# A four-layer graph network on one core: where the exponential stands in ScalarE's order of the attention pass

## The reference

```python
def _top_p_attention(X, W1, W2, W3):
    q = X @ W1.T @ W2.T
    k = X @ W3.T
    probs = softmax(q @ k.T, axis=-1)                  # 5000 x 5000
    # keep the largest probabilities of each row until their sum reaches 0.9
    ...
    return A / A.sum(-1, keepdims=True)

R = S + eye(N);  R = R / R.sum(-1)                     # S is the adjacency
for n in range(2):
    A  = _top_p_attention(Xa, W1, W2, W3)
    Xf = R @ Xf                                        # "diffusion"
    Xa = A @ Xa                                        # "attention"
    Z  = Z + Xf @ U1[n].T + Xa @ U2[n].T
h = X + Z                                              # then layer norm, gain and bias
```

## Time and profile before

| what | value |
|---|---|
| device time, median of 3 runs | 7562.4 us |
| device time, lowest and highest | 7555.11 and 7564.21 us |
| device time of the profiled execution | 7571.29 us |
| its span, first to last instruction | 7569.5 us |
| granted PE clock, mean over the span | 0.830 |
| first attention pass, about | 747 to 1984 us |
| second attention pass, about | 2153 to 5397 us |

### The profile page before, as it was taken

One profiled execution on the slowest core, in us unless ns is written; L12 is line 12 of the kernel. 1 busy time (PEld: TensorE's weight loads), 2 busy tenths in 40 slices (PEclk: granted clock), 3 DMA queues, 4 the chain that ended last, 5 costly groups with the idle time before them and its releaser, 6 DMA issues. The chain is left out here.

```text
span 7569.5 us, 83686 instructions
## 1 busy us (share of the span) xinstructions
PE 4816.2 (64%) x27812; PEld 3349.8 (44%) x27812; DVE 5526.4 (73%) x13021; ACT 2216.4 (29%) x2953; POOL 297.3 (4%) x170
## 2 busy tenths in 40 slices
PE   5994888888674365524375477753316888853981
PEld 2442566666554354413264466643312222212981
DVE  4883677777348888887877778778445999974864
ACT  2332555555310011101032233321204222212541
POOL 0000000000110000000000000000000210220000
PEclk9996788888888697867687788877658999986995
DMA  5550000000032121201111111110011333312850
GB/s 173 200 201 19 1 2 1 2 1 1 26 121 88 54 90 72 80 28 42 53 69 45 39 69 70 69 52 31 21 36 65 109 103 114 109 57 75 301 186 27
DMA packets 192724, 549.73 MB, mean 73 GB/s; under 512 B 20026, under 2 KB 77125, under 8 KB 192125
## 3 DMA queue, kind: packets, MB, share of 16 engines
q1 hardware_dynamic: 187069, 539.58, 20.0%
q0 software_dynamic: 5120, 3.97, 0.2%
HBM read 526.73 MB, written 16.68 MB: 72 GB/s over the span
## 5 line engine op out<-in xcount | busy, mean ns | idle before, releaser
L647 PE MATMUL ps<-ident,arena 125*125 125x125 f32 x3200 | 544.1, 304 | 1223.4 <-DVEq L1098 1223.4
L655 PE MATMUL ps<-arena,turned 125*125 125x129 f32 x6400 | 951.0, 299 | 196.8 <-ACT turned L750 196.8
L679 PE MATMUL ps<-arena 125*125 125x129 f32 x6400 | 833.3, 290 | 318.7 <-DMA arena<-in_adj_tiles 311.6
L647 PEld LDWEIGHTS ps<-ident,arena 125*125 125x125 f32 x3200 | 475.6, 217 | 1262.5 <-DVEq L1098 1236.6
L750 ACT ACTIVATE turned<-ps 125x500 f32<-125x500 f32 x800 | 463.5, 585 | 1876.0 <-PE ps L647 1875.2
L1382 DVE SCALAR_TENSOR_TENSOR arena<-arena,pair 125x1000 f32<-125x1000 f32 x800 | 939.3, 1250 | 71.0 <-ACT arena L1345 71.0
L655 PEld LDWEIGHTS ps<-arena,turned 125*125 125x125 f32 x6400 | 876.8, 210 | 209.8 <-ACT turned L750 205.4
L679 PEld LDWEIGHTS ps<-arena 125*125 125x125 f32 x6400 | 781.3, 199 | 391.0 <-DMA arena<-in_adj_tiles 307.4
L1400 PE MATMUL ps<-arena 125*64 125x500 f32 x3200 | 763.8, 601 | 193.9 <-DVE arena L1382 193.9
L640 PE MATMUL ps<-arena,wt 64*125 64x500 f32 x1600 | 724.9, 608 | 11.0 <-ACT wt L728 9.5
L1064 DVE SCALAR_TENSOR_TENSOR arena<-arena,wt 125x5000 f32<-125x5000 f32 x80 | 434.1, 5427 | 311.6 <-issue 311.6
(11 more groups left out here) (343 smaller groups left out, 5904.3 us busy)
## 6 DMA issues: line engine op xcount, KB each, us to landing
arena<-in_adj_wide SPq DMA_DIRECT2D x400, 500.0 KB, 4.5
arena<-in_adj_tiles SPq DMA_DIRECT2D x400, 488.3 KB
arena<-in_adj_wide SPq DMA_DIRECT2D x100, 1000.0 KB, 4.8
x_saved<-arena SPq DMA_DIRECT2D x4, 2500.0 KB
arena<-x_saved SPq DMA_DIRECT2D x3, 2500.0 KB
arena<-att_saved SPq DMA_DIRECT2D x1, 2519.5 KB
arena<-in_x SPq DMA_DIRECT2D x1, 2500.0 KB
arena<-in_h SPq DMA_DIRECT2D x1, 2500.0 KB
```

The costliest lines, as they stand in the source:

```text
L647: mm = pe.transpose(banks_turn[:, g % 2, c * P:(c + 1) * P], work[b % DEPTH][:, j:j + P], ident[0:P, 0:P])
L655: mm = pe.matmul(acc_attend, turned[:, g % 2, c * P:(c + 1) * P], nodes(v_attend, FA)[:, j, :], start=(j == 0), stop=(j == NB - 1))
L679: mm = pe.matmul(acc_spread, ring[:, j * P:(j + 1) * P], values[:, j, :], start=(j == 0), stop=False)
```

## The change

In ScalarE's order of a round, in both passes, `exponentials(b + 1)` now stands between `take(b - 1)` and `copy_logits(b + 2)`. Before, it stood behind `copy_logits(b + 2)`. No instruction is added or removed, and the orders of the other engines stay as they are.

```diff
                         if b > 0:
                             take(b - 1)
+                        if b + 1 < NB:
+                            exponentials(b + 1)
                         if b + 2 < NB:
                             copy_logits(b + 2)
-                        if b + 1 < NB:
-                            exponentials(b + 1)
                         if spreads:
                             for n in in_block(b):
                                 keep_diffused(n)
```

## The result

The changed kernel takes 7601.7 us in the median of 5 runs (7594.7 to 7603.9), the kernel before 7564.2 in 5 runs beside it. The ratio is 1.0050, with a 95% interval of 1.0036 to 1.0064: 37 us slower, where I had forecast 42 us faster. The profiled execution has a span of 7602.1 us against 7569.5.

The account below looks back on a forecast made before the run. It took ACT, with PE answering it, to bound the first pass at 30.0 us a round, DVE next at 28.9. The median of 7562.4 less DVE's 42.4 us wait gave 7520 us, range 7508 to 7548.

Parts of the forecast that it names:

- The bound and the wait: First pass: ACT with PE sets rounds of 30.0 us against DVE's 28.9; DVE's 42.4 us wait for the exponential goes.
- ACT's ring: First pass: closed cycle of ACT's work, answered by PE group by group, without slack; 30.0 us a round, 27.5 after.
- The order on ACT and PE: First pass: exponential at the take's end without waiting for maxima; PE stalls about 2.5 us after four groups of logits.
- the price of the low clock in the logits: First pass logits: the stall brings a low-clock spell, priced as 3.4 us of work at half speed, 1.7 us.
- the sum: First pass round on ACT: 13.8 us from take's end to query copy, 0.2 to next take, less 2.5 saved.
- rival D: First pass: the stall lowers the clock for the remaining logits every round; rounds 32.5 us, total 7652 us; chance 0.09.
- The hint against it: PE's logits: by the skill's rule, short idle times between groups cycling through PSUM banks cost clock; no size given.
- The margins on DVE: First pass: last logit copy done at about 29.3 us after `keep(b - 1)`, wanted at some 36; no new wait.
- Rival E: Second pass slower because PE's 2.4 us a round reach DVE; 40 us, total 7560; chance 0.08 together with no change.
- I take nothing for it: Second pass: PE leaves its logits 2.4 us later each round, margin 3 us and more, so no effect was counted.

## Why the prediction was wrong, point by point

**The bound and the wait.** Right. ACT's ring was the longer one at 30.0 us a round, and DVE's own share, which I put at 28.9 us, is 28.76 to 28.79 in all kernels that took the wait away. The 42 us of waits were there to be had: three kernels gained 34 to 43.

**The order on ACT and PE.** Right: a stall of 2.19 us where I had 2.5, four groups ahead of it, and no wait of the exponential for the maxima. The take, for which I allowed up to 2.4 us less than 16.0, is 14.2 to 15.6 us, 14.9 in the mean.

**The step that failed is the price of the low clock in the logits**, "3.4 us of work at half speed, 1.7 us". I read the length of the spell from the diffusion in the earlier trace rows, where 3 us were low behind a stall of 2.65 us. (The 1.7 us hold for a spell of 3.4 us, half of which is lost; 3.4 us of work at half speed would cost 3.4 more.) Here the spell is 13.7 or 17.1 us long around each stall of 2.19 us. It covers all six groups that are left or, as in the round shown, all but the first of them, at 0.84 us more for each, and reaches into the take.

In the terms of the sum: from the take's end to the next take I had 13.8 + 0.2 - 2.5 = 11.5 us, and 13.2 with the 1.7. It is 16.7, so the low clock cost about 5.2 us and not 1.7. With the 14.9 us of the take that is the ring of 31.6 us. This is rival D, to which I gave 0.09. D put the ring at 27.5 + 5.0 = 32.5 us with the take as slow as before, and the whole at 7652; the take was 1.1 us shorter. My reason against D was that the spell in rows 8 was short and that the take would speed up. The take did speed up, and D held all the same, because its margin was 2.5 us and the logits alone cost twice that.

The 37 us by which the kernel is slower flatter the prediction: the order in the first pass, the only place where it saw an effect, costs 55 us where it had 42 the other way. The 18.5 us of the second pass, which it put at nothing, hide a third of that.

**The hint against it.** The rule of the Trainium skill on idle times between groups that cycle through PSUM banks (TensorE: Matmul & The Clock Gate, "A second HAM failure mode: psum-queue depth-cycling") describes this case: its logits cycle through four banks, and 2.19 us of idle time a round went with 14.5 us at the low clock. I took the size of the loss from a stretch of another kind. In the first pass itself, the kernel before had a low spell of 6.8 us in every round, twice what I priced.

**The margins on DVE.** The copies were to be done 7 us before DVE wanted them. That sum had the clock high. With the groups behind the stall at 1.67 us the last copy is late, and L819 waits group by group. The sum also had the take begin 2 us after `keep(b - 1)`, which holds only where DVE is the longer one; in the round shown it begins at 939.42, 9.8 us after L1064 ended at 929.66, as it was 9.5 us before.

**The second pass.** Rival E, a loss, did not come: L1084 does not wait there. But "I take nothing for it" was wrong in the other sense. I worked out that PE would reach the diffusions later and asked only whether DVE would wait for PE. I did not ask what the tiles, which are loaded as PE frees the ring, run beside. In the second pass alone the change is 18.5 us faster, for a reason that the prediction doesn't have; had the first pass been neutral, "faster" would have come true by luck.

## What to carry to other kernels

When a move in one engine's order opens a stall in PE, price it first at the low clock for all that follows the stall in the round, and call the change a gain only if it survives that; or place the moved work where PE's free banks cover the rest of its group, as behind the sixth of ten copies here. Idle time with no releaser ahead of a branch is worth a look beside the DMA queues: it may be code that waits behind data. Where a step moves another engine's transfers, ask what they will then run beside.

## What the runs showed of the hardware

- A stall of 2.19 us in each round of 31.6 us went with 13.7 us at the low clock in 26 of 34 rounds and 17.1 us in 8, at least twice the 6.8 us that went with the longer idle time of 5.31 us in each round of the kernel before. Three added products in that stall held the clock at 1.00 through the logits of all 34 rounds. What decides the length of such a spell was not tried further.
- DVE's way over a branch to L1064 cost 1.24 us of idle time in rounds without an instruction packet and about 3.5 us in rounds with one and the data queue silent. In the round shown with 125 GB/s of tiles beside it, it cost 6.7 us; 7.0 was the most. L1064 started 1.8 to 2.4 us after the start of the packet in all of these.
